# GpSimd's gate products: eight tensor_scalar instructions become two affine selections

## The chip, the cores and the metric

One NeuronCore of a Trainium2 chip runs the whole program. The metric is the device time of one execution in microseconds (us). The engines are TensorE (PE in the rows, PEld for its weight loads), VectorE (DVE), ScalarE (ACT), GpSimd (POOL) and SyncE (SP, which here only issues DMAs).

## The reference

`x` is `[8, 256, 256]` f32. The output is `x + attention(norm(x)) + experts(norm(x))`.

```python
# gated delta rule, 32 value heads, 16 key heads, chunks of 128 tokens; g is the log of the decay
g = -exp(A_log) * softplus(a + dt_bias)
def step(state, (q_t, k_t, v_t, g_t, b_t)):
    state = state * exp(g_t)
    delta = (v_t - state^T k_t) * b_t
    state = state + k_t delta^T
    return state, state^T q_t
y = rmsnorm(out * silu(z)) * norm_w @ w_out
# experts: 8 heads, the best 8 of 2048 experts for each token and head
z = silu((h . down_embed[indices]) * softmax(sc))
out = sum(z * up_embed[indices])
```

The kernel does not step through tokens: inside a chunk of 128 tokens it needs the matrix of decays `exp(g_{j+1} + ... + g_i)` for every pair of tokens. The exponent is made by one matrix product per four tasks: a constant triangle of ones (`C_GT`, row index greater than column index) times the matrix `gm[p, i] = g_p if p <= i else 0`. This `gm` is what the change is about.

## The kernel before

A first stage (up to about 284 us) normalises `x`, runs the dense part of the experts, finds the experts' indices and computes the gates `gates[:, 3, ...]`, which hold g for all tokens. Then come 64 passes. Pass `n` (with `f = n + 1`) does two things at once: the front half of the attention for group `f` (four head pairs' chunks, eight tasks `a`, each a 128x128 matrix), and the back half for group `n`, together with 16 expert slots of one tile of 128 tokens: a gather of 16 rows per token and the products with them.

Each engine has its own instruction list, in the order of the program text; they meet through semaphores. What matters here in one pass:

- GpSimd, `one_pass` of `block.gpsimd`: copies `cols2` (L964) and `xr` (L966), then, once TensorE has read the last `gm` (semaphore `diff_t`), `gate_sums(f + 1)` (L935 copies eight columns of g to `gn`; L939 makes the eight matrices of `gm`, a constant triangle `mask(C_LE)` times a column of `gn`). Then it waits for VectorE's third masked level (`e_v`, 3), copies the 16 indices (`picks`, L943) and `h2c` (L973), issues eight indirect DMAs (`gather(0)`, L952), scales the attention's output (`finish`, L928 and L931), waits for `mix_v`, issues the other eight gathers, computes `norm` (L980) and `MT` (L984, two instructions).
- VectorE, `one_pass` of `block.vector`: waits until all 16 rows have landed (`gathered`), runs 16 `expert_dot` (L1193: `rows` times `h2c`, summed; each is followed by a read of the accumulator), `zc` (L1299), the second half of the outputs (L1153, L1147), the masked level 0 (L1165 twice), part of the weighted sum of rows (L1204, L1207, L1210), three convolution taps (L1177), and the masked level 1 (L1165), whose first instruction raises `e_v` to 3.
- TensorE's `differences(g)` (L527) reads `gm` at the beginning of the next pass, after `gm_p` has reached its last value.

So `gm` is made one pass ahead, in a stretch in which VectorE is at the dot products.

Of the kernel before, what the change touches and what calls it, by code (L numbers as in the profile page):

```python
# [33 lines left out]
ALU = mybir.AluOpType  # L34
# [3 lines left out]
P = 128  # L38
# [6 lines left out]
TASKS = 8  # L45
# [13 lines left out]
C_ID, C_LE, C_GT, C_SU, C_EYE, C_MS = 0, 1, 2, 3, 4, 6  # L59
# [20 lines left out]
def program(nc, x, wkq, wvz, ckq, cvv, woh, wba, dtb, alog, nw, wup, bup, wdn, bdn, wq, keys, table, consts, out):  # L80
    ctx = ExitStack()
    with ctx:
        def sb(name, shape, dt=F32):
            return ctx.enter_context(nc.sbuf_tensor(name, shape, dt))

        def sem(name):
            return ctx.enter_context(nc.semaphore(name))
# [9 lines left out]
        h2_all = sb("h2_all", [P, TILES, P])  # L97
# [5 lines left out]
        def mask(c, n=1):  # L103
            m = cst[:, c * P:(c + 1) * P]
            return m if n == 1 else m.unsqueeze(1).broadcast_to([P, n, P])
# [29 lines left out]
        def diagonal(s):  # L135
# [7 lines left out]
                 "diff_t exp_done kk_t ss_t v_t e_t x_t xt_t proj_t y0_t s_t o0_t ks_t y1_t o1_t "  # L143
                 "yt_t out_t silu_s sq_s rv_s x_s xt_s tap_s z_s S_s qs_s sumsq_s yT_s "
                 "km_v kq_v ssk_v s_v at_v e_v conv_v ys0_v r1_v ys1_v xg_v acc_v rms_v elim_v dot_v "
                 "gn_p gm_p cols_p pick_p norm_p mt_p rms_p y_p zero_p scal_step silu_e sim_v mix_v "
                 "h2_s gate_v gate_s").split()
        sm = {n: sem(n) for n in names}
        nums = [s.num for s in sm.values()]
# [4 lines left out]
        class Step:  # L154
# [10 lines left out]
            def wait(self, n=None):  # L165
# [4 lines left out]
                   y1_t=1, o1_t=1, out_t=2, silu_e=1, exp_done=2, tap_s=8, x_s=4, xt_s=6, silu_s=4, sq_s=2, sumsq_s=8,  # L170
                   rv_s=8, S_s=1, qs_s=4, z_s=2, yT_s=2, dot_v=1, xg_v=4, e_v=6, conv_v=4, km_v=1, kq_v=1, ssk_v=2,
                   s_v=1, at_v=2, rms_v=1, mix_v=1, elim_v=1, ys0_v=2, ys1_v=2, r1_v=4, acc_v=2, cols_p=1, zero_p=1,
                   gn_p=1, gm_p=8, rms_p=1, y_p=8, pick_p=1, norm_p=1, mt_p=2, w_vz=32, xb_in=16, wo_in=16, w_kq=32,
                   blocks_out=32, blocks_in=16, inv_out=32, inv_in=64)
        place = {"u": 0}

        def at(name, n):

            return place["u"] * per[name] + n

        def last(name, n=None):

            return (place["u"] - 1) * per[name] + (per[name] if n is None else n)
# [55 lines left out]
        gn = sb("gn", [P, TASKS])  # L239
        gm = sb("gm", [P, TASKS, P])  # L240
# [51 lines left out]
        h2c = sb("h2c", [P, P])  # L292
# [5 lines left out]
        def task(b, c, r):  # L298
            return (2 * b + c) * R + r
# [104 lines left out]
        def _(pe):  # L404
# [99 lines left out]
            def one_pass(f, nx, back):  # L504
# [76 lines left out]

                if not back:
                    pe.wait_ge(loaded_kq, 32)
                    pe.wait_ge(sm["gm_p"], at("gm_p", 8))
                if place["u"] and front:
                    pe.wait_ge(sm["gm_p"], last("gm_p"))
                    pe.wait_ge(sm["z_s"], last("z_s", 1))
# [324 lines left out]
        def _(pool):  # L912
# [12 lines left out]
            def finish():  # L925

                pool.wait_ge(sm["rms_v"], at("rms_v", 1))
                pool.tensor_tensor(rms[:, :], rms[:, :], minus_half, ALU.pow).then_inc(sm["rms_p"], 1)  # L928
                pool.wait_ge(sm["rms_p"], at("rms_p", 1))
                for a in range(TASKS):  # L930
                    pool.tensor_scalar(xg[:, a, :], xg[:, a, :], rms[:, a:a + 1], None, ALU.mult).then_inc(sm["y_p"], 1)  # L931

            def gate_sums(f, calls=1):

                pool.tensor_copy(gn[:, :].rearrange("p (t r) -> p t r", t=4),  # L935
                                 gates[:, 3, bass.ds(4 * (f // HEADS), 4), bass.ds(R * (f % HEADS), R)]).then_inc(sm["gn_p"], 1)
                pool.wait_ge(sm["gn_p"], at("gn_p", calls))
                for a in range(TASKS):
                    pool.tensor_scalar(gm[:, a, :], mask(C_LE), gn[:, a:a + 1], None, ALU.mult).then_inc(sm["gm_p"], 1)  # L939

            def picks(f):

                pool.tensor_copy(pick[:, :], idx_all[:, bass.ds(f // 4, 1), bass.ds((f % 4) * 16, 16)].rearrange("p a c -> p (a c)"))\  # L943
                    .then_inc(sm["pick_p"], 1)

            def gather(k0):

                pool.wait_ge(sm["pick_p"], at("pick_p", 1))
                for k in range(k0, k0 + K // 2):
                    for s in range(2):  # L950
                        m = K * s + k
                        pool.indirect_dma_start(rows[:, m, :], None, table[:, :],  # L952
                                                bass.IndirectOffsetOnAxis(ap=pick[:, m:m + 1], axis=0)).then_inc(gathered, 16)

            def one_pass(f, nx, n):

                if f is None:
                    finish()
                    return
                hn, pn = f % HEADS, f // HEADS  # L960
                if place["u"]:
                    pool.wait_ge(sm["qs_s"], last("qs_s"))
                    pool.wait_ge(sm["inv_out"], last("inv_out"))
                pool.tensor_copy(cols2[nx][:, :, :].rearrange("p q (t r) -> p q t r", t=4),  # L964
                                 gates[:, 0:3, bass.ds(4 * pn, 4), bass.ds(R * hn, R)]).then_inc(sm["cols_p"], 1)
                pool.tensor_copy(xr[:, 0:BL * BL], cst[0:NB * TASKS, C_EYE * P:(C_EYE + 2) * P]).then_inc(sm["zero_p"], 1)  # L966
                pool.wait_ge(sm["diff_t"], at("diff_t", 2))
                if f + 1 < PASSES:
                    gate_sums(f + 1, 2 if n is None else 1)
                if n is not None:  # L970
                    pool.wait_ge(sm["e_v"], at("e_v", 3))
                picks(f)
                pool.tensor_copy(h2c[:, :], h2_all[:, bass.ds(f // 4, 1), :].rearrange("p a c -> p (a c)"))  # L973
                gather(0)
                if n is not None:
                    finish()
                    pool.wait_ge(sm["mix_v"], at("mix_v", 1))
                gather(K // 2)
                pool.wait_ge(sm["ssk_v"], at("ssk_v", 2))
                pool.tensor_tensor(norm2[nx][:, :], ss[:, :, :].rearrange("p w t -> p (w t)"), both, ALU.pow).then_inc(sm["norm_p"], 1)  # L980
                pool.wait_ge(sm["exp_done"], at("exp_done", 2))
                pool.wait_ge(sm["kq_v"], at("kq_v", 1))
                for g in range(2):
                    pool.tensor_tensor(MT2[nx][:, 4 * g:4 * g + 4, :].rearrange("p (t r) i -> p t r i", r=R),  # L984
                                       kq[:, 2 * g:2 * g + 2, :].unsqueeze(2).broadcast_to([P, 2, R, P]),
                                       DT[:, 4 * g:4 * g + 4, :].rearrange("p (t r) i -> p t r i", r=R), ALU.mult).then_inc(sm["mt_p"], 1)
# [23 lines left out]
        def _(dve):  # L1010
# [139 lines left out]
            def second_outputs(st, nx):  # L1150

                qs = QS[:, :, :].rearrange("p b d -> p (b d)")
                st.did(V.tensor_tensor(qs, ps[:, 4, :], qs, ALU.add))  # L1153
                st.wait()
                gated(1, qs, rq2[nx], z2[nx])

            def one_pass(nx, n, st, front=True):
# [5 lines left out]
                def level(lv, g):  # L1163
                    dve.wait_ge(sm["e_t"], at("e_t", 2 * lv + g + 1))
                    V.tensor_tensor(E[:, 4 * g:4 * g + 4, :], ps[:, g, :].rearrange("p (a i) -> p a i", a=4), mask(C_MS + lv, 4), ALU.mult)\  # L1165
                        .then_inc(sm["e_v"], 1)
# [25 lines left out]
                def expert_dot(k):  # L1192
                    st.did(V.tensor_tensor_reduce(out=rows[:, k, 0:P], in0=rows[:, k, 0:P], in1=h2c[:, :], scale=1.0, scalar=0.0,  # L1193
                                                  op0=ALU.mult, op1=ALU.add, accum_out=dot[:, k:k + 1]))
# [96 lines left out]
                if back:  # L1291
                    total = acc[:, bass.ds(n // 4, 1), :].rearrange("p a d -> p (a d)")
                    dve.wait_ge(gathered, 256 * n + 256)
                    for k in range(16):
                        expert_dot(k)

                    st.wait()
                    pr = prob_all[:, bass.ds(n // 4, 1), bass.ds((n % 4) * 16, 16)].rearrange("p a c -> p (a c)")
                    V.tensor_tensor(zc[:, 0, :], dot[:, :], pr, ALU.mult).then_inc(sm["dot_v"], 1)  # L1299
                    if place["u"]:  # L1300
                        dve.wait_ge(sm["o1_t"], last("o1_t"))
                        dve.wait_ge(sm["qs_s"], last("qs_s"))
                        dve.wait_ge(sm["z_s"], last("z_s"))
                        dve.wait_ge(sm["norm_p"], last("norm_p"))
                        dve.wait_ge(sm["mt_p"], last("mt_p"))
                    second_outputs(st, nx)
                    level(0, 0)
                    level(0, 1)
                    dve.wait_ge(sm["silu_e"], at("silu_e", 1))
                    expert_mix(0, 3)  # L1310
# [46 lines left out]
                if back:  # L1357
                    dve.wait_ge(sm["ks_t"], at("ks_t", 1))
                    for b in range(2):
                        for r in range(R):  # L1360
                            a = task(b, 1, r)
# [67 lines left out]
```

## Time and profile before

| | |
|---|---|
| median of 3 runs | 3440.19 us (3438.79 to 3451.68) |
| the profiled execution's own time | 3440.67 us |
| its span (first to last instruction) | 3438.8 us |
| busy: PE / PEld / DVE / ACT / POOL | 2992.4 / 2451.1 / 3012.3 / 1794.2 / 2306.0 us |
| POOL L939 `gm` | 512 instructions, 362.9 us |
| POOL L952 gathers | 1024 instructions, 1157.2 us |
| DVE L1193 dot products | 1024 instructions, 342.9 us |

The table gives busy time per engine and per group of instructions. Busy time says nothing of what a group delays: for that one needs the chain that ended last and, for one pass, the timelines of the two engines side by side.

### The profile page before, as it was taken

The page shows a single profiled execution, that of the slowest core. Times are in us where ns is not written, and L with a number is a line of the kernel's source. Part 1 is how long each engine was busy: PE and PEld are TensorE (multiplying, and loading weights), DVE is VectorE, ACT ScalarE, POOL GpSimd, SP SyncE. Part 2 cuts the span into 40 slices and gives each one's busy share as a digit, 9 for nine tenths or more (in the row PEclk, how much of TensorE's full clock was granted, in tenths as well). Part 3 has the DMA queues.
Part 4 walks back from the last instruction along what each step waited for, and adds up shares of the span by engine and source line. Part 5 has one row for each costly group of instructions (what it writes and reads, how often), then busy time and mean ns, then how long its engine had stood idle before and what let it go on. Part 6 is the DMA issues. An engine that isn't in the chain of part 4 may idle for free.

```text
span 3438.8 us, 56504 instructions
## 1 busy us (share of the span) xinstructions
PE 2992.4 (87%) x18444; PEld 2451.1 (71%) x18444; DVE 3012.3 (88%) x9101; ACT 1794.2 (52%) x4111; POOL 2306.0 (67%) x2650
## 2 busy tenths in 40 slices
PE   7844999989998989899989988898989899998997
PEld 4422777778776777677767777777777777777776
DVE  5996999989998999899989898998899898989996
ACT  3322555555554555455545555555555555555553
POOL 0005777777767776777778777877777667877764
PEclk9976999999999999999999999999999999999999
DMA  1003545544555545454545554544555454544553
GB/s 60 1 1 104 137 132 141 135 131 132 137 139 135 131 133 139 130 133 133 141 126 138 134 138 124 149 127 134 138 138 137 125 139 132 146 129 135 144 132 89
DMA packets 541827, 427.98 MB, mean 124 GB/s; under 512 B 247008, under 2 KB 450784, under 8 KB 541536
## 3 DMA queue, kind: packets, MB, share of 16 engines
q1 hardware_dynamic: 476000, 222.98, 24.0%
q0 software_dynamic: 65536, 201.39, 22.0%
q8 instruction: 149, 2.44, 0.3%
q14 instruction: 142, 1.16, 0.1%
HBM read 345.61 MB, written 45.09 MB: 114 GB/s over the span
## 4 chain that ended last, share of the span: by engine, by line
DVE 36%; POOL 35%; PE 14%; issue 9%; DMA 5%; ACT 1%; SPq 0%; DVEq 0%; POOLq 0%; ACTq 0%
POOL rows L952 22%; DVE rows L1193 9%; POOL xg L931 9%; DVE qkv L1177 6%; DVE mix L1210 4%; POOL rms L928 3%; DVE E L1165 3%; DMA rows<-table,pick 3%; PE ps L579 3%; PE ps L500 3%; PE ps L517 2%; PE ps L665 1%; DVE topi L1024 1%; DVE xg L1147 1%; PE ps L521 1%
## 5 line engine op out<-in xcount | busy, mean ns | idle before, releaser
L952 POOL DMA_INDIRECT rows<-table,pick x1024 | 1157.2, 1130 | 326.3 <-issue 326.3
L551 PE MATMUL ps<-X,AT 128*128 128x128 f32 x3072 | 417.7, 294 | 119.2 <-DMA XT<-whole 119.2
L551 PEld LDWEIGHTS ps<-X,AT 128*128 128x128 f32 x3072 | 392.9, 207 | 169.8 <-DMA XT<-whole 167.3
L806 ACT ACTIVATE qkv<-qkv 128x512 f32<-128x512 f32 x256 | 161.5, 631 | 518.6 <-DVE qkv L1177 518.6
L571 PE MATMUL ps<-XT,E 128*128 128x128 f32 x3072 | 400.6, 277 | 0.0
L801 ACT ACTIVATE raw<-ps 128x512 f32<-128x512 f32 x256 | 152.8, 597 | 433.2 <-PE ps L517 433.2
L1210 DVE SCALAR_TENSOR_TENSOR mix<-rows,zc,mix 128x256 f32<-128x256 f32 x896 | 375.1, 476 | 0.0
L571 PEld LDWEIGHTS ps<-XT,E 128*128 128x128 f32 x3072 | 368.9, 192 | 0.0
L939 POOL TENSOR_SCALAR gm<-cst,gn 128x128 f32<-128x128 f32 x512 | 362.9, 723 | 6.7
L1193 DVE CUSTOM_DVE_ANT_0 rows<-rows,h2c 128x128 f32<-128x128 f32 x1024 | 342.9, 399 | 9.2 <-SPq L328 4.7
L931 POOL TENSOR_SCALAR xg<-xg,rms 128x128 f32<-128x128 f32 x520 | 324.9, 637 | 7.0
L564 PEld LDWEIGHTS ps<-E,XT 128*128 128x128 f32 x2048 | 257.7, 193 | 98.1 <-DVE E L1165 56.5
L1177 DVE SCALAR_TENSOR_TENSOR qkv<-raw,cwv,qkv 128x510 f32<-128x510 f32 (+2 forms) x384 | 307.7, 802 | 6.8
L1177 DVE SCALAR_TENSOR_TENSOR qkv<-raw,cwkq,qkv 128x510 f32<-128x510 f32 (+2 forms) x384 | 285.7, 744 | 21.4 <-ACT qkv L802 12.1
L564 PE MATMUL ps<-E,XT 128*128 128x128 f32 x2048 | 274.1, 277 | 26.4 <-DVE E L1165 26.4
L943 POOL COPY pick<-idx_all 128x16 uint32<-128x16 uint32 x64 | 12.6, 196 | 421.9 <-DVE E L1165 421.9
L816 ACT ACTIVATE XT<-ps 128x512 f32<-128x512 f32 x384 | 228.0, 594 | 94.3 <-PE ps L571 86.4
L517 PE MATMUL ps<-xnT,Wkq 128*128 128x512 f32 x512 | 273.6, 661 | 0.0
L1165 DVE TENSOR_TENSOR E<-ps,cst 128x512 f32<-128x512 f32 x384 | 253.2, 682 | 14.6 <-PE ps L551 9.1
L517 PE MATMUL ps<-xnT,Wvz 128*128 128x512 f32 x512 | 254.2, 622 | 0.0
L500 PE MATMUL ps<-wo,yT 128*128 128x256 f32 x1040 | 247.6, 382 | 0.0
L521 PE MATMUL ps<-Wvz,xb 128*128 128x256 f32 x1024 | 243.1, 381 | 0.0
(167 smaller groups left out, 6333.4 us busy)
## 6 DMA issues: line engine op xcount, KB each, us to landing
Wvz<-wvz SPq DMA_DIRECT2D x64, 512.0 KB, 3.3
xb<-xnT SPq DMA_DIRECT2D x64, 512.0 KB, 4.4
whole<-AT SPq DMA_DIRECT2D x128, 256.0 KB, 3.6
X<-whole SPq DMA_DIRECT2D x128, 256.0 KB, 3.9
XT<-whole SPq DMA_DIRECT2D x128, 256.0 KB, 4.4
wo<-woh SPq DMA_DIRECT2D x65, 256.0 KB, 4.4
Wkq<-wkq SPq DMA_DIRECT2D x64, 256.0 KB, 2.5
rows<-table,pick POOLq DMA_INDIRECT x1024
```

What stands on the lines that cost most here:

```text
L500: done = mm(ps[:, 2 + g, c * D:(c + 1) * D], yT[:, task(g, c, r), :], wo[:, r, :], start=r == 0, stop=r == R - 1)
L517: done = mm(ps[:, bank, :], w[:, k, :], xnT[:, k, bass.ds(pn * N, N)], start=k == 0, stop=k == KD - 1)
L551: done = mm(ps[:, g, (a % 4) * P:(a % 4 + 1) * P], AT_b[:, a, :], src[:, a, :], start=True, stop=True)
L564: done = mm(ps[:, 2 + g, (a % 4) * P:(a % 4 + 1) * P], src[:, a, :], E[:, a, :], start=True, stop=True)
L571: done = mm(ps[:, 4 + g, (a % 4) * P:(a % 4 + 1) * P], E[:, a, :], src[:, a, :], start=True, stop=True)
L931: pool.tensor_scalar(xg[:, a, :], xg[:, a, :], rms[:, a:a + 1], None, ALU.mult).then_inc(sm["y_p"], 1)
L939: pool.tensor_scalar(gm[:, a, :], mask(C_LE), gn[:, a:a + 1], None, ALU.mult).then_inc(sm["gm_p"], 1)
L952: pool.indirect_dma_start(rows[:, m, :], None, table[:, :], bass.IndirectOffsetOnAxis(ap=pick[:, m:m + 1], axis=0)).then_inc(gathered, 16)
L1165: V.tensor_tensor(E[:, 4 * g:4 * g + 4, :], ps[:, g, :].rearrange("p (a i) -> p a i", a=4), mask(C_MS + lv, 4), ALU.mult)\
L1177: ins = V.scalar_tensor_tensor(out=o, in0=i, scalar=w, in1=o, op0=ALU.mult, op1=ALU.add)
L1193: st.did(V.tensor_tensor_reduce(out=rows[:, k, 0:P], in0=rows[:, k, 0:P], in1=h2c[:, :], scale=1.0, scalar=0.0, op0=ALU.mult, op1=ALU.add, ...
L1210: sums[s] = st.did(V.scalar_tensor_tensor(out=mix[:, s, :], in0=rows[:, m, P:ROW], scalar=zc[:, 1, m:m + 1], in1=mix[:, s, :], op0=ALU.mul ...
```

## The change

`gate_sums` fills the same `gm` with two instructions in place of eight. Each takes four columns of `gn`, broadcasts every one over 128 columns (a stride of zero), and keeps the element where `column - partition >= 0`, else writes 0. The constant triangle is no longer read. The semaphore `gm_p` rises by 2 in a pass in place of 8. A register for the fill value is set once ahead of the passes. GpSimd's copy to `h2c` now raises a semaphore `h2c_p`, and VectorE waits for its value of the pass before, ahead of the dot products.

```diff
@@ block.gpsimd
+            zero = pool.to_reg(0.0)
             def gate_sums(f, calls=1):
                 pool.tensor_copy(gn[:, :].rearrange("p (t r) -> p t r", t=4),
                                  gates[:, 3, bass.ds(4 * (f // HEADS), 4), bass.ds(R * (f % HEADS), R)]).then_inc(sm["gn_p"], 1)
                 pool.wait_ge(sm["gn_p"], at("gn_p", calls))
-                for a in range(TASKS):
-                    pool.tensor_scalar(gm[:, a, :], mask(C_LE), gn[:, a:a + 1], None, ALU.mult).then_inc(sm["gm_p"], 1)
+                for g in range(2):
+                    pool.affine_select(gm[:, 4 * g:4 * g + 4, :], gn[:, 4 * g:4 * g + 4].unsqueeze(2).broadcast_to([P, 4, P]),
+                                       [[0, 4], [1, P]], ALU.is_ge, zero, base=0, channel_multiplier=-1).then_inc(sm["gm_p"], 1)
@@ one_pass
-                pool.tensor_copy(h2c[:, :], h2_all[:, bass.ds(f // 4, 1), :].rearrange("p a c -> p (a c)"))
+                pool.tensor_copy(h2c[:, :], h2_all[:, bass.ds(f // 4, 1), :].rearrange("p a c -> p (a c)")).then_inc(sm["h2c_p"], 1)
@@ block.tensor, one_pass
-                    pe.wait_ge(sm["gm_p"], at("gm_p", 8))
+                    pe.wait_ge(sm["gm_p"], at("gm_p", 2))
@@ block.vector, one_pass
                     dve.wait_ge(gathered, 256 * n + 256)
+                    if place["u"]:
+                        dve.wait_ge(sm["h2c_p"], last("h2c_p"))
                     for k in range(16):
                         expert_dot(k)
```

## Rows read from the trace of the kernel before

**Rows 1.** The page: span, busy time of each engine, shares of the chain.

```profile
span 3438.8 us, 56504 instructions
...
DVE 36%; POOL 35%; PE 14%; issue 9%; DMA 5%; ACT 1%; SPq 0%; DVEq 0%; POOLq 0%; ACTq 0%
```

**Rows 2.** GpSimd's waits: waiter <- releaser: us in total, times, longest.

```profile
POOL pick L943 <- DVE E L1165: 421.9, 63, 13.2
```

**Rows 3.** The chain in 2025 to 2045 us: start, us, what.

```profile
2025.08 4.12 DMA rows<-table,pick
...
2034.84 0.06 DVE zc L1299
...
2034.95 0.05 DVEq L1305
...
2043.23 0.61 DVE E L1165
```

**Rows 4.** GpSimd's timeline of the same pass: start, us, instruction, idle before.

```profile
2028.15 2.48 POOL L984 TENSOR_TENSOR MT<-kq,DT 128x512 f32<-128x512 f32 x2
2030.59 0.19 POOL L964 COPY cols<-gates 128x24 f32<-128x24 f32 x1
2030.74 0.39 POOL L966 COPY xr<-cst 64x256 f32<-64x256 f32 x1
...
2031.43 5.74 POOL L939 TENSOR_SCALAR gm<-cst,gn 128x128 f32<-128x128 f32 x8
2043.90 0.20 POOL L943 COPY pick<-idx_all 128x16 uint32<-128x16 uint32 x1 [6.73 <-DVE E L1165]
```

**Rows 5.** VectorE's timeline of the same pass.

```profile
2027.81 1.28 DVE L1142 TENSOR_TENSOR acc<-acc,ps 128x512 f32<-128x512 f32 x2
2029.22 2.06 DVE L1193 CUSTOM_DVE_ANT_0 rows<-rows,h2c 128x128 f32<-128x128 f32 x1
...
2031.63 0.28 DVE L1193 CUSTOM_DVE_ANT_0 rows<-rows,h2c 128x128 f32<-128x128 f32 x1
...
2031.85 0.36 DVE L1193 CUSTOM_DVE_ANT_0 rows<-rows,h2c 128x128 f32<-128x128 f32 x1
...
2034.01 0.36 DVE L1193 CUSTOM_DVE_ANT_0 rows<-rows,h2c 128x128 f32<-128x128 f32 x1
```

**Rows 6.** GpSimd's groups by shape: busy us, mean ns.

```profile
L939 POOL TENSOR_SCALAR gm<-cst,gn 128x128 f32<-128x128 f32 x512 | 362.9, 723 | 6.7
L984 POOL TENSOR_TENSOR MT<-kq,DT 128x512 f32<-128x512 f32 x128 | 159.2, 1260 | 0.0
L966 POOL COPY xr<-cst 64x256 f32<-64x256 f32 x64 | 24.8, 387 | 0.0
L973 POOL COPY h2c<-h_all 128x128 f32<-128x128 f32 x64 | 18.8, 293 | 0.0
```

**Rows 7.** VectorE's groups by shape.

```profile
L1142 DVE TENSOR_TENSOR acc<-acc,ps 128x512 f32<-128x512 f32 x130 | 83.1, 679 | 12.3 <-PE ps L500 12.3
L1147 DVE SCALAR_TENSOR_TENSOR xg<-QS,norm,z 128x256 f32<-128x256 f32 x130 | 65.0, 539 | 2.3
L1147 DVE SCALAR_TENSOR_TENSOR xg<-ps,norm,z 128x256 f32<-128x256 f32 x128 | 56.0, 479 | 197.5 <-PE ps L579 197.5
L1153 DVE TENSOR_TENSOR QS<-ps,QS 128x512 f32<-128x512 f32 x65 | 45.0, 692 | 2.4 <-issue 0.4
```

**Rows 8.** L939: duration ns min/median/max, first and last start.

```profile
L939 POOL TENSOR_SCALAR gm<-cst,gn x512: 595/738/1131, 284.4 to 3296.0; 128x128 f32<-128x128 f32 x171
```

**Rows 9.** GpSimd's timeline of a longer pass, and VectorE's first dot product there.

```profile
2088.15 5.45 POOL L939 TENSOR_SCALAR gm<-cst,gn 128x128 f32<-128x128 f32 x8
2099.16 0.20 POOL L943 COPY pick<-idx_all 128x16 uint32<-128x16 uint32 x1 [5.57 <-DVE E L1165]
...
2086.44 0.28 DVE L1193 CUSTOM_DVE_ANT_0 rows<-rows,h2c 128x128 f32<-128x128 f32 x1
```

**Rows 10.** The chain in 280 to 336 us, ahead of the passes.

```profile
284.44 4.67 POOL gm L939 x8
```

More of the change, by code:

```diff
@@ L145, in program @@
                  "km_v kq_v ssk_v s_v at_v e_v conv_v ys0_v r1_v ys1_v xg_v acc_v rms_v elim_v dot_v "
-                 "gn_p gm_p cols_p pick_p norm_p mt_p rms_p y_p zero_p scal_step silu_e sim_v mix_v "
+                 "h2c_p gn_p gm_p cols_p pick_p norm_p mt_p rms_p y_p zero_p scal_step silu_e sim_v mix_v "
                  "h2_s gate_v gate_s").split()
@@ L172, in program @@
                    s_v=1, at_v=2, rms_v=1, mix_v=1, elim_v=1, ys0_v=2, ys1_v=2, r1_v=4, acc_v=2, cols_p=1, zero_p=1,
-                   gn_p=1, gm_p=8, rms_p=1, y_p=8, pick_p=1, norm_p=1, mt_p=2, w_vz=32, xb_in=16, wo_in=16, w_kq=32,
+                   h2c_p=1, gn_p=1, gm_p=2, rms_p=1, y_p=8, pick_p=1, norm_p=1, mt_p=2, w_vz=32, xb_in=16, wo_in=16, w_kq=32,
                    blocks_out=32, blocks_in=16, inv_out=32, inv_in=64)
```

## The prediction

> **What bounds the kernel now.** I read the page first for the span and the shares of the chain, then GpSimd's waits, then the chain of one pass in the middle, and at last the timelines of GpSimd and VectorE over that pass, side by side. The chain belongs to two engines in turn, VectorE with 36% and GpSimd with 35% [rows 1]. The waits show how they take turns: 63 times, once a pass, GpSimd stands still for 421.9 us in all until VectorE's masked level is written, and only then copies the indices [rows 2]. In the pass read here the gather's data lands at 2029.20 [rows 3], VectorE's first dot product starts at 2029.22 [rows 5], VectorE works without a real gap to the end of the masked level at about 2043.85 [rows 3], and GpSimd's index copy starts at 2043.90 [rows 4]. From there GpSimd carries the chain again (gathers, output scaling, gathers). So a pass is a loop of a VectorE stretch and a GpSimd stretch.
>
> The eight gate products lie in neither. They run on GpSimd from 2031.43 to 2037.17, while VectorE has the turn, and behind them GpSimd is idle for 6.73 us [rows 4]. Their own 362.9 us [rows 6] are therefore not on the path. What they can change is how fast VectorE gets through its stretch, and that is the whole question here.
>
> **What GpSimd does to VectorE in that stretch.** The first dot product took 2.06 us where its neighbours take 0.28 [rows 5]. It ended at 2031.28, so it really ran from 2031.00. From 2029.22 to 2031.00 it was held, while GpSimd was in its two MT instructions (to 2030.63), the copy of cols and the copy of xr (to 2031.13) [rows 4]. Two things follow. A GpSimd instruction that reads this memory holds a VectorE instruction with two such inputs (rows and h2c). And it isn't let in between GpSimd instructions that follow each other closely: the two copies have one input each, and still kept it out 0.37 us after MT's end. Instructions of VectorE that take one input from PSUM don't suffer: the two additions to acc, from 2027.81, lay largely beside MT and took 1.28 us together [rows 5], no more than their group's mean of 679 ns each, and QS<-ps,QS, of the same shape, has 692 though it lies beside the gate products [rows 7].
>
> The gate products hold VectorE only a little: in this pass four of the dot products took 0.36 in place of 0.28, one for each gate product that ran beside them (at 2031.85, 2032.57, 2033.29 and 2034.01; the first and the last stand in [rows 5]). One gate product takes 595 ns at least [rows 8], but costs VectorE only 0.08; most of it is spent on something else than reading 128 elements.
>
> The Trainium skill has a rule for this, on the page "SBUF — State Buffer", section "SBUF: two separate sides": GpSimd and VectorE lock a shared pair of ports, one excludes the other for the whole instruction, and a VectorE instruction with two SBUF inputs is one that needs it. The MT rows agree (held 1.78 us); the gate products' rows don't agree as to the whole instruction (0.08 of 0.6 us). By the rule to the letter, eight products held it for their whole length and two selections would hold it for less, which speaks for the change; by the rows it speaks against.
>
> **The change part by part.**
>
> 1. Taken out: what the eight products cost VectorE in its stretch. Four dot products by 0.08 is 0.32. The two xg instructions have a mean of 539 ns with QS as source, and 479 with PSUM as source in another place of the pass [rows 7]: 2 x 0.06 = 0.12. Together 0.45 us a pass. There are 512/8 = 64 sets of products, two of them ahead of the first pass (the first at 284.4), so 62 passes gain: 62 x 0.45 = 28 us.
>
> 2. Put in: what two selections of 512 elements cost VectorE. The trace has no affine selection on any engine, so I bound it. They begin where the products began, 2031.43, and there are 12 or 13 dot products left (zc follows them at 2034.84 [rows 3]), each with two inputs, so everything that the pair holds hits VectorE. Length from below: a copy on GpSimd takes 293 ns for 128 elements and 387 for 256, so 0.73 ns an element and 0.2 us fixed [rows 6]; at 512 it would be 0.57 us, 1.15 for the pair. From above: MT, also 512 elements written but with two inputs, takes 1.26 [rows 6], or 2.5 for the pair; per element (1.26 - 0.2)/512 = 2.07 ns. The selection reads one input as the copy does, but has to form an index and compare for each element. I take the middle of the two rates, 1.4 ns: 0.2 + 0.72 = 0.91 us, 1.83 for the pair. As with MT, cols and xr I take it that VectorE isn't let in between the two; the dot product that is already running at the start gives back about 0.2. So VectorE is held for 1.65 us a pass (with the copy's rate 0.95, with MT's 2.3).
>
> The Trainium skill prices such a loop: "GPSIMD Engine Reference", section "Performance pitfalls for Q7 kernels", gives 2.03 cycles an element for compare and select, not unrolled, at the 1.2 GHz of its "Specifications". As an estimate from that page this is 0.87 us for 512 elements, 1.07 with the fixed 0.2, and the sum below would come to about 3530 us. No row here shows it.
>
> 3. Net: 1.65 - 0.45 = +1.20 us in a pass. All of it lands on the path, since VectorE's stretch has no gap to take it up and GpSimd's index copy waits for its end: 62 x 1.20 = +74 us. In the few longer passes, as the one at 2086, the products begin 1.71 us after the first dot product [rows 9]; eight or nine dot products are still to come, so it holds there too.
>
> 4. GpSimd ends gate_sums earlier, by 5.74 - 1.83 = 3.9 us. Nothing waits for that: its idle time before the index copy grows from 6.7 to about 11.8 us (6.7 + 3.9 + 1.2). TensorE reads gm only in the next pass.
>
> 5. Ahead of the first pass the eight products are on the chain once, with 4.67 us [rows 10]. The pair needs 1.83: -2.8 us. The second set there has its length hidden by the front half of the first pass.
>
> 6. The wait for h2c_p asks for a copy of the pass before, long done. It stands behind the wait for the gather, ahead of the first dot product. Another step of VectorE's queue on the chain costs 0.05 us [rows 3]; in the usual pass the first dot product is held by MT until 2031.00 anyway, which hides it. Without that cover it would be 63 x 0.05 = 3 us; I put in 0. Setting the register for zero once: 0. TensorE's wait for 2 in place of 8 asks for the same moment.
>
> Sum, against the profiled execution's own time: 3440.67 + 74 - 2.8 = 3512 us. The median of the runs shown, 3440.19, is 0.5 below it, so this is also the forecast for the median. With the copy's rate: 0.95 - 0.45 = 0.50, x 62 = 31, less 3.5: 3468. With MT's: 1.85 x 62 = 115, less 2.2: 3553.
>
> **The rivals.**
>
> A. The selection holds VectorE only for a read at the rate seen with the products, 0.08 us for each 128 elements, and lets it in between. Then 8 x 0.08 = 0.64 against 0.45: +0.19 x 62 = +12, less 2.8, or 3450 us. For it: the products are of that kind, 0.6 us long and holding for a seventh of that. Against it: MT and both copies were not.
>
> B. The selection doesn't hold VectorE at all, or no longer than the products did for the whole set, because it makes most of its values itself and its input is only four numbers a partition. VectorE gets back the 0.45 us: -28 - 3 = 3410 us, faster. It decides wherever the pair holds VectorE for less than 0.45 us. For it: the input has a stride of zero. Against it: the copy of xr, a plain one-input instruction, held it nearly to its end.
>
> C. The selection is a slow loop, slower than MT. If it takes what four products take without contention, 4 x 0.595 = 2.4 us [rows 8], and holds the port for it, VectorE loses 4.5 us a pass: 4.05 x 62 = +251, or about 3690 us. For it: tensor_scalar with a column as its scalar takes 595 ns for 128 elements, far above a copy's 293, so GpSimd's loops differ much. Against it: much of that seems to be fixed cost. GpSimd's own slack decides only beyond 5.74 + 6.73 = 12.5 us for the pair [rows 4], which I leave out.
>
> D. That the products are gone from GpSimd and the time falls because GpSimd is 35% of the chain: excluded, since the idle time behind them is there in the usual pass and in the longer one (6.73 and 5.57 us) [rows 4, 9].
>
> **How the numbers follow.** Within 0.5% (17 us) counts as no change here, about what a measurement of this kernel can tell. The forecast (pair held for between 0.95 and 2.3 us) has a chance of 0.60, with a range of its own of 3465 to 3555; A 0.15; B 0.13; C with all between MT's rate and it 0.12. Faster: B, 0.13. Same: A without its slower end, 0.14. Slower: 0.60 + 0.12 and A's rest, 0.73. The range leaves out B (0.13) and the upper part of C (0.07), and reaches from 3438 to 3620 us. The predicted time is that of the forecast, 3512.
>
> **What would show it.** In the profile after: a selection's mean between 0.57 and 1.26 us; GpSimd's wait for VectorE's masked level up from 421.9 to about 740 us (63 waits, about 5 us each more); in a usual pass one or two dot products besides the first that last 0.8 to 2 us, and the other dot products all at 0.28; xg<-QS at about 480 ns; the stretch from the first dot product to the index copy longer by 1.2 us, and the stretch from there to the next gather's landing unchanged. The forecast is wrong if no dot product besides the first is over 0.4 us (then B or A), if the held dot products add up to more than 2.5 us a pass (C), or if VectorE's stretch grows and the span doesn't, which would mean that the loop isn't closed as I read it.

## The result, and the profile after

The changed kernel takes 3471.17 us (median of 5 runs, 3469.07 to 3483.47), the kernel before 3442.12 in the same comparison. The ratio is 1.0088, with a 95% interval of 1.0064 to 1.0112: slower by 29 us, where the forecast was slower by 71. The sign and the place are as predicted, the size isn't.

The page of the changed kernel: span, busy time of each engine.

```profile
span 3473.8 us, 56184 instructions
PE 3002.3 (86%) x18444; PEld 2449.5 (71%) x18444; DVE 3041.1 (88%) x9101; ACT 1796.4 (52%) x4111; POOL 2022.8 (58%) x2266
```

GpSimd got 283 us less to do (2306.0 before) and the kernel got slower. Its waits show where the 283 us went:

```profile
POOL pick L946 <- DVE E L1168: 721.2, 63, 12.4
```

It was 421.9 [rows 2], so GpSimd waits 299 us more. The next two fences are the timelines of GpSimd and of VectorE in one usual pass; they answer to [rows 4] and [rows 5].

```profile
2051.75 2.49 POOL L987 TENSOR_TENSOR MT<-kq,DT 128x512 f32<-128x512 f32 x2
2054.19 0.19 POOL L967 COPY cols<-gates 128x24 f32<-128x24 f32 x1
2054.34 0.39 POOL L969 COPY xr<-cst 64x256 f32<-64x256 f32 x1
2054.68 0.24 POOL L937 COPY gn<-gates 128x8 f32<-128x8 f32 x1
2055.00 1.27 POOL L941 TENSOR_SCALAR_AFFINE_SELECT gm<-gn 128x512 f32<-128x512 f32 x2
2067.94 0.20 POOL L946 COPY pick<-idx_all 128x16 uint32<-128x16 uint32 x1 [11.67 <-DVE E L1168]
```

```profile
2052.74 2.15 DVE L1196 CUSTOM_DVE_ANT_0 rows<-rows,h2c 128x128 f32<-128x128 f32 x1
2054.81 0.28 DVE L1196 CUSTOM_DVE_ANT_0 rows<-rows,h2c 128x128 f32<-128x128 f32 x1
2055.02 0.76 DVE L1196 CUSTOM_DVE_ANT_0 rows<-rows,h2c 128x128 f32<-128x128 f32 x1
2055.71 0.70 DVE L1196 CUSTOM_DVE_ANT_0 rows<-rows,h2c 128x128 f32<-128x128 f32 x1
2056.35 0.28 DVE L1196 CUSTOM_DVE_ANT_0 rows<-rows,h2c 128x128 f32<-128x128 f32 x1
```

The pair lasts 1.27 us, and beside it stand exactly two long dot products, 0.76 and 0.70 in place of 0.28: 0.48 + 0.42 = 0.90 us held. All later ones take 0.28. The first of the two ends at 2055.78, while GpSimd's pair is still running, so VectorE does get in between the two selections; the second ends 0.14 us behind the pair. GpSimd then idles for 11.67 us. In the groups by shape, the xg instructions with QS as source took 539 ns before [rows 7] and take 484 now, nearly the 479 of those with PSUM as source; QS<-ps,QS, which has one input from PSUM, took 692 ns and takes 691:

```profile
L1150 DVE SCALAR_TENSOR_TENSOR xg<-QS,norm,z 128x256 f32<-128x256 f32 x130 | 57.6, 484 | 2.3
L1156 DVE TENSOR_TENSOR QS<-ps,QS 128x512 f32<-128x512 f32 x65 | 44.9, 691 | 2.8 <-issue 0.8
```

To follow this through all passes I cut each of the 62 passes that make a gm at two moments that can be read in any timeline: the end of the first dot product, and the start of GpSimd's index copy. Between them lies VectorE's stretch, from there to the next pass's first dot product lies GpSimd's.

| | VectorE's stretch, median | sum over 62 | GpSimd's stretch, median | sum over 62 |
|---|---|---|---|---|
| before | 12.62 us | 785.1 | 34.94 us | 2219.7 |
| changed | 13.06 us | 811.5 | 34.97 us | 2221.4 |

VectorE's stretches account for 26.4 us and GpSimd's for 1.7. The profiled execution is 35 us longer than the one before; most of the rest, 8 us, lies ahead of the first pass, where TensorE's granted clock had a mean of 0.86 in the first 100 us against 1.00 in the execution before. In another profile of the changed kernel (below) that clock is 1.00 and the first dot product ends 9.6 us earlier. Over all thirteen profiles of this document the first dot product ends at 331 to 335 us where that clock is 1.00, at 339 to 342 where it is 0.93, and at 342 and 343 where it is 0.86, whatever the kernel. So these 8 us belong to the execution and not to the change.

### The profile page after: what moved, and what is told of

Read it like the earlier page. It is cut to its first block, busy times and chain, and to the rows that moved or that the text cites. A ratio compares the mean times of both kernels' runs of the same rounds, so it can differ in the third digit from the quotient of the medians.

```text
span 3473.8 us, 56184 instructions
## 1 busy us (share of the span) xinstructions
PE 3002.3 (86%) x18444; PEld 2449.5 (71%) x18444; DVE 3041.1 (88%) x9101; ACT 1796.4 (52%) x4111; POOL 2022.8 (58%) x2266
## 3 DMA queue, kind: packets, MB, share of 16 engines
q14 instruction: 140, 1.15, 0.1%
## 4 chain that ended last, share of the span: by engine, by line
DVE 37%; POOL 36%; PE 12%; issue 10%; DMA 5%; ACT 0%; DVEq 0%; SPq 0%; POOLq 0%; ACTq 0%
POOL rows L955 23%; DVE rows L1196 10%; POOL xg L931 9%; DVE qkv L1180 6%; DVE mix L1213 4%; DMA rows<-table,pick 4%; DVE E L1168 3%; POOL rms L928 3%; PE ps L500 2%; PE ps L579 2%; PE ps L517 2%; DVE topi L1027 1%; DVE QS L1156 1%; DVE xg L1150 1%; PE ps L665 1%
## 5 line engine op out<-in xcount | busy, mean ns | idle before, releaser
L946 POOL COPY pick<-idx_all 128x16 uint32<-128x16 uint32 x64 | 12.7, 198 | 721.2 <-DVE E L1168 721.2
L1196 DVE CUSTOM_DVE_ANT_0 rows<-rows,h2c 128x128 f32<-128x128 f32 x1024 | 373.9, 429 | 11.6 <-SPq L328 5.6
L517 PE MATMUL ps<-xnT,Wkq 128*128 128x512 f32 x512 | 265.6, 644 | 0.0
L1150 DVE SCALAR_TENSOR_TENSOR xg<-ps,norm,z 128x256 f32<-128x256 f32 x128 | 56.0, 479 | 204.8 <-PE ps L579 204.8
```

Of the source, the lines that this page charges most:

```text
L517: done = mm(ps[:, bank, :], w[:, k, :], xnT[:, k, bass.ds(pn * N, N)], start=k == 0, stop=k == KD - 1)
```

## Experiments

Theory P is the prediction's, with its size put right by the profile: two selections hold VectorE's two-input instructions for 0.45 us each, where the products cost 0.45 us for the whole set. Rival W: the cost is the new semaphore and wait. Rival L: GpSimd's instruction list falls differently, and more passes are long ones. In every seventh or so of the passes GpSimd stands still for 4 to 6 us ahead of one of its indirect DMAs, for no reason that the profile shows (longest 6.1 us). In the pass of [rows 9], which follows such a stop, VectorE reaches its first dot product at 2086.44, when MT and the two copies have been over since 2082.68. I count a pass as long where the first dot product isn't held, that is, takes under 0.4 us: 8 of 62 before, 11 in the changed kernel.

Beside the first eight experiments the kernel before takes about 3500 us, beside the last three 3447. The number of the chip doesn't tell the two groups apart: it is 3 for four of the eight (the wait alone, one column, late selections, late products) and for the last three, and 9 for the other four. The cause of the difference is open. In the slower group all kernels have a GpSimd stretch of 35.6 to 35.8 us, 0.7 more than above, and 21 to 28 long passes. VectorE's median stretch is the same in both groups where the two can be compared (12.62 for the kernel before and for the wait alone), which makes it the better measure; its sum over the 62 passes stands beside it, since a median hides a minority of longer passes. "Held" is what the 15 later dot products of a pass take above 0.28 us, median over the passes.

| | ratio to before (95%) | VectorE's stretch, median | sum over 62 | held |
|---|---|---|---|---|
| before (again) | 0.9989 (0.9974 to 1.0003) | 12.62 | 784.7 | 0.34 |
| changed (again) | 1.0076 (1.0058 to 1.0093) | 13.07 | 810.9 | 0.90 |
| wait alone | 1.0012 (0.9988 to 1.0035) | 12.62 | 782.2 | 0.34 |
| selections of one column | 0.9952 (0.9929 to 0.9975) | 12.19 | 766.1 | 0.04 |
| eight selections of 128 | 1.0082 (1.0052 to 1.0112) | 12.86 | 798.2 | 0.70 |
| one selection of 1024 | 1.0100 (1.0070 to 1.0131) | 13.09 | 815.2 | 0.93 |
| three selections of 512 | 1.0227 (1.0195 to 1.0259) | 13.49 | 845.1 | 1.33 |
| products late | 0.9958 (0.9934 to 0.9983) | 12.38 | 770.6 | 0.01 |
| selections late | 0.9917 (0.9886 to 0.9949) | 12.22 | 762.1 | 0.05 |
| selections late, again | 0.9949 (0.9926 to 0.9973) | 12.21 | 759.8 | 0.00 |
| selections and copies late | 0.9906 (0.9891 to 0.9922) | 12.22 | 778.2 | 0.00 |

**The wait alone.** The kernel before with the semaphore only.

```diff
-                pool.tensor_copy(h2c[:, :], ...)
+                pool.tensor_copy(h2c[:, :], ...).then_inc(sm["h2c_p"], 1)
                     dve.wait_ge(gathered, 256 * n + 256)
+                    if place["u"]:
+                        dve.wait_ge(sm["h2c_p"], last("h2c_p"))
```

> The kernel before with nothing of the change but its semaphore: GpSimd's copy to h2c raises h2c_p, VectorE waits for it ahead of the dot products. Theory P (the two selections hold VectorE's dot products for about 0.45 us each, 0.90 a pass, where the eight products and their effect on xg cost 0.45 a pass): the wait is hidden, 3442 us, ratio to before 0.999 to 1.001, spans and dot products as before (four of 0.36 us a pass). Rival W (the new wait and semaphore are the cost): about 3470 us, ratio 1.008. Rival L (the list of GpSimd's instructions falls differently, so that more passes are long ones, 11 against 8): 3442, since its list is as before.

Measured 1.0012, an interval across 1, and VectorE's stretch is 12.62 us as before. W falls.

**Selections of one column.** Every instruction and semaphore of the change, nearly nothing to read.

```diff
+                w = P if n is None else 1
                 for g in range(2):
-                    pool.affine_select(gm[:, 4 * g:4 * g + 4, :], gn[:, 4 * g:4 * g + 4].unsqueeze(2).broadcast_to([P, 4, P]),
-                                       [[0, 4], [1, P]], ...)
+                    pool.affine_select(gm[:, 4 * g:4 * g + 4, 0:w], gn[:, 4 * g:4 * g + 4].unsqueeze(2).broadcast_to([P, 4, w]),
+                                       [[0, 4], [1, w]], ...)
```

> The changed kernel, but inside the passes each of the two selections fills one column of each of its four matrices in place of 128; the rest of gm is left as it was (this leaves out the fill of the later passes, so the decays are wrong). All instructions and semaphores stay. Theory P: nothing holds the dot products any more, they all take 0.28 us but the first of a pass, VectorE's stretch is 0.90 us shorter than in the changed kernel and 0.45 shorter than before: 3442 - 28 - 3 = 3411 us, ratio 0.991. W and L: as the changed kernel, about 3470, ratio 1.008.

VectorE's stretch is 12.19 us, 0.43 below before and 0.87 below the changed kernel: this is the stretch with nearly nothing beside it (held 0.04), and it gives both terms of the sum. The products cost 12.62 - 12.19 = 0.43 us a pass, the two selections 13.06 - 12.19 = 0.87. The time fell by less than the 27 us that this is worth (62 x 0.43): the ratio is 0.9952, and 0.991 lies outside its interval. In its profile VectorE's stretches add up to 766 us, 16 below the 782 of the wait alone, since 12 of its 62 passes have one of 12.5 us or more (up to 14.5); GpSimd's add up to 2297 us against 2277, with 26 long passes against 23. So a part of the gain was given back on both sides; why stays open.

**Eight selections of 128, and one of 1024.** The same elements in other pieces; the same instruction, once with `for a in range(TASKS)` over `gm[:, a, :]`, once over all of `gm`.

```diff
-                for g in range(2):
-                    pool.affine_select(gm[:, 4 * g:4 * g + 4, :], gn[:, 4 * g:4 * g + 4].unsqueeze(2).broadcast_to([P, 4, P]), [[0, 4], [1, P]], ...)
+                for a in range(TASKS):
+                    pool.affine_select(gm[:, a, :], gn[:, a:a + 1].broadcast_to([P, P]), [[1, P]], ...)
```

> The changed kernel with eight selections of 128 columns in place of two of 512: the same elements, the same input. Theory P1 (what holds VectorE is the time that a selection reads, at one element a cycle or about 0.83 ns, 0.43 us for 512): each lasts about 0.3 us and holds by up to 0.11; together 0.6 to 0.9 us a pass, VectorE's stretch 12.8 to 13.1 us, ratio 1.005 to 1.009. Rival P2 (a selection holds nearly from its start to its end, fixed part included, 0.2 of 0.64 us more each): 8 x 0.3 = up to 2 us a pass, stretch 14 us, ratio above 1.02.

> The changed kernel with one selection of 1024 columns. Theory P1: 1.07 us long (0.2 + 1024 x 0.83 ns), one dot product held by 0.85 to 0.90 us, no other; stretch 13.0 to 13.1 us as with two, ratio 1.007 to 1.009. If reading ahead into a queue frees VectorE before the selection ends, the hold is well under 0.85 us and the ratio under 1.005.

The selections' own lines (duration ns min/median/max), first of the changed kernel, then with 128 and with 1024 columns:

```profile
L941 POOL TENSOR_SCALAR_AFFINE_SELECT gm<-gn x128: 636/641/682, 292.7 to 3327.6; 128x512 f32<-128x512 f32 x128
```

```profile
L941 POOL TENSOR_SCALAR_AFFINE_SELECT gm<-gn x512: 287/337/520, 290.1 to 3389.5; 128x128 f32<-128x128 f32 x171
```

```profile
L940 POOL TENSOR_SCALAR_AFFINE_SELECT gm<-gn x64: 1091/1091/1097, 290.2 to 3413.6; 128x1024 f32<-128x1024 f32 x64
```

From 512 to 1024 elements a selection grows by 0.45 us, 0.88 ns an element; about 0.19 us are fixed. VectorE beside the one of 1024, and then beside the eight of 128:

```profile
2090.61 1.21 DVE L1195 CUSTOM_DVE_ANT_0 rows<-rows,h2c 128x128 f32<-128x128 f32 x1
2091.76 0.28 DVE L1195 CUSTOM_DVE_ANT_0 rows<-rows,h2c 128x128 f32<-128x128 f32 x1
```

```profile
2090.29 0.41 DVE L1196 CUSTOM_DVE_ANT_0 rows<-rows,h2c 128x128 f32<-128x128 f32 x1
...
2090.93 0.36 DVE L1196 CUSTOM_DVE_ANT_0 rows<-rows,h2c 128x128 f32<-128x128 f32 x1
```

One dot product held by 0.93, or eight of them by 0.08 (the first by 0.13). Theory P1 had expected 0.85 to 0.90 for the one, and up to 0.11 each for the eight; both stretches lie in their ranges, and the stretch of 14 us of P2 falls. The ratio of the 1024, 1.0100, is just above its range. For the eight the ratio of 1.0082 is higher than the stretch of 12.86 is worth: (12.86 - 12.62) x 62 is 15 us, or 0.4%.

Which part of a selection holds isn't settled by this. P1 says its reading part, about 0.9 us per 1024 elements: that is 0.93 of 1.09 us for the one, and 0.11 where 0.08 of 0.29 was measured for each of the eight. But a hold up to the selection's end, with one dot product let in between two selections, fits as well or better. The selection of 1024 runs from 2090.59 to 2091.68 and the held dot product ends 0.14 us later, and so it is beside the selections of 512 and of 128: the median over their held dot products is 0.14 us each time. Free dot products follow each other every 0.21 us (2054.81, 2055.02 above). If each selection costs its own length less one such step, that gives 1.09 - 0.21 = 0.88, 0.64 - 0.21 = 0.43 and 0.29 - 0.21 = 0.08 us, where 0.93, 0.45 and 0.08 were measured. P2 had left out the dot product let in. No run separates the two accounts, and both give nearly the same price.

This shows also that a product isn't cheaper to VectorE than a selection of the same size: one of 128 elements holds by 0.08 [rows 5], as a selection of 128 does. Of a product, though, most lets VectorE through: beside each of the first four products in the pass of [rows 4], 0.72 to 0.88 us long, there are three or four dot products, and only one of them is held. What differed between eight products and eight selections is how they lay. The products were spread over 5.7 us, from 2031.43 to 2037.17, and the last ones fell beside these VectorE instructions of before, of which QS and E have an input from PSUM; the eight selections lie in 2.35 us, all beside dot products.

```profile
2035.05 0.69 DVE L1153 TENSOR_TENSOR QS<-ps,QS 128x512 f32<-128x512 f32 x1
2035.77 1.01 DVE L1147 SCALAR_TENSOR_TENSOR xg<-QS,norm,z 128x256 f32<-128x256 f32 x2
2036.70 1.27 DVE L1165 TENSOR_TENSOR E<-ps,cst 128x512 f32<-128x512 f32 x2
```

**Three selections of 512.** A third one into a buffer that nobody reads.

```diff
+                if n is not None:
+                    if place["u"]:
+                        pool.wait_ge(sm["ex_p"], last("ex_p"))
+                    pool.affine_select(gx[:, :, :], gn[:, 0:4].unsqueeze(2).broadcast_to([P, 4, P]),
+                                       [[0, 4], [1, P]], ...).then_inc(sm["ex_p"], 1)
```

> The changed kernel with a third selection of 512 columns behind the two in every pass, into a buffer that nobody reads. GpSimd has over 11 us of idle time for it. Theory P, with what the first runs showed (a selection of 512 columns lasts 0.64 to 0.66 us and holds one dot product by 0.45): three held dot products a pass in place of two, VectorE's stretch from the end of the first dot product to GpSimd's index copy 13.51 us in place of 13.06, the whole 28 us above the changed kernel, ratio to before about 1.017. If the cost is no matter of the selections (W, L): ratio 1.008 and a stretch of 13.06.

```profile
2120.64 0.76 DVE L1202 CUSTOM_DVE_ANT_0 rows<-rows,h2c 128x128 f32<-128x128 f32 x1
2121.33 0.70 DVE L1202 CUSTOM_DVE_ANT_0 rows<-rows,h2c 128x128 f32<-128x128 f32 x1
2121.96 0.70 DVE L1202 CUSTOM_DVE_ANT_0 rows<-rows,h2c 128x128 f32<-128x128 f32 x1
```

Three held dot products, and a stretch of 13.49 us where 13.51 was expected. The ratio, 1.0227, is above the 1.017 expected, outside its interval. Its profile has 28 long passes against 22 in the second one of the late selections (below), taken on the same chip, and its GpSimd stretches add up to 2303 us against 2281. In this group of runs a longer VectorE stretch costs somewhat more than its own length; the cause is open.

**Late.** GpSimd has over 11 us of slack behind the selections, so they may be moved to where VectorE has an input from PSUM. One wait does that, for the selections and, in a kernel of its own, for the eight products of before:

```diff
                 pool.wait_ge(sm["gn_p"], at("gn_p", calls))
+                if n is not None:
+                    pool.wait_ge(sm["xg_v"], at("xg_v", 2))
```

> The changed kernel, with one more wait on GpSimd: the two selections of a pass (not the copy of gn ahead of them) wait until VectorE has written both of its second outputs xg (xg_v, 2), so that they lie beside the two masked levels E<-ps, which take one input from PSUM and last 1.2 us together. Theory P: dot products at 0.28, xg at 0.48, the levels unaffected, the first mix instruction held by 0.1 to 0.2 us: 3442 - 28 - 3 + 9 = 3420 us, ratio 0.991 to 0.995, faster than both. W and L: about 3470. If GpSimd holds every VectorE instruction and not only those with two inputs in SBUF: 3470 too, with E<-ps at 0.9 to 1.1 us.

GpSimd and VectorE with the late selections:

```profile
2069.40 1.23 POOL L943 TENSOR_SCALAR_AFFINE_SELECT gm<-gn 128x512 f32<-128x512 f32 x2 [5.14 <-DVE xg L1152]
2076.43 0.20 POOL L948 COPY pick<-idx_all 128x16 uint32<-128x16 uint32 x1 [5.80 <-DVE E L1170]
```

```profile
2068.38 0.88 DVE L1152 SCALAR_TENSOR_TENSOR xg<-QS,norm,z 128x256 f32<-128x256 f32 x2
2069.18 1.28 DVE L1170 TENSOR_TENSOR E<-ps,cst 128x512 f32<-128x512 f32 x2
2070.37 0.53 DVE L1209 SCALAR_TENSOR_TENSOR mix<-rows,zc,acc 128x256 f32<-128x256 f32 x1
```

The same two selections, the same wait for h2c, and the cost is gone: the two E take 1.28 us as in the changed kernel, where nothing lay beside them, and only the end of the second selection holds a mix, 0.53 against 0.47. Stretch 12.22, ratio 0.9917. W can't give that, and L says nothing of a shorter VectorE stretch (the long passes are 22, about as many as the 23 of the wait alone). A hold of every VectorE instruction is excluded too.

> The two selections made to wait for VectorE's second outputs, once more, to see if it beats both kernels again: stretch 12.22 us against 12.62 before and 13.06 changed, 62 x 0.40 = 25 us and 3 us ahead of the passes: ratio to before 0.992, with 0.988 to 0.996 allowed for runs in which more passes are long ones.

Again faster: 0.9949, stretch 12.21.

> The kernel before, with the same wait ahead of its eight products. They last 4.8 to 5.7 us and so cannot hide beside the two levels of 1.2 us. Theory P: the dot products are free (0.32 us gained), xg too (0.12), but about six products run beside mix and the convolution taps and cost 0.08 to 0.1 us each: 3435 to 3445 us, ratio 0.998 to 1.001. If products cost VectorE nothing beside those instructions: 3414. The late gm itself has no price: GpSimd has 6.7 us of idle time there and uses about 5.5 of it.

```profile
L941 POOL TENSOR_SCALAR gm<-cst,gn x512: 592/800/1154, 284.0 to 3349.6; 128x128 f32<-128x128 f32 x171
```

The dot products are free (held 0.01), the stretch is 12.38: the products still cost 12.38 - 12.19 = 0.19 us beside mix and the taps, less than expected (six products at 0.08 to 0.1, about 0.5). The mix group's mean went from 476 to 507 ns, but the three taps beside them took 0.77, 0.75 and 0.75 us, two of them as undisturbed. The ratio is 0.9958 where 0.998 to 1.001 was expected; 62 x 0.24 = 15 us, or 0.4%, is what the stretch is worth. GpSimd pays instead: its median product went from 738 ns [rows 8] to 800.

**Selections and copies late.** The first dot product of a usual pass is held by MT, cols and xr. The two copies can wait as well.

```diff
+                if n is not None:
+                    pool.wait_ge(sm["dot_v"], at("dot_v", 1))
                 pool.tensor_copy(cols2[nx][:, :, :] ...
```

> The late selections, and the copies of cols and xr wait too, until VectorE's dot products are done (dot_v), so that they lie beside QS<-ps,QS, which has an input from PSUM. Theory P: the first dot product of a usual pass is let in at the end of MT, not 0.37 us behind it, so the stretch from GpSimd's index copy to the end of the first dot product is 0.3 to 0.4 us shorter in the passes where MT holds it (40 of 62 or so), the stretch behind it stays 12.22: 15 us below the late selections, ratio to before 0.988 to 0.991. Rival: the copies are not what keeps the dot product out, it needs 0.37 us to start behind MT: ratio 0.992 to 0.995 as with the late selections alone.

```profile
2019.71 2.49 POOL L991 TENSOR_TENSOR MT<-kq,DT 128x512 f32<-128x512 f32 x2
2025.91 0.20 POOL L971 COPY cols<-gates 128x24 f32<-128x24 f32 x1 [3.72 <-DVE zc L1308]
2026.06 0.39 POOL L973 COPY xr<-cst 64x256 f32<-64x256 f32 x1
2027.53 1.23 POOL L943 TENSOR_SCALAR_AFFINE_SELECT gm<-gn 128x512 f32<-128x512 f32 x2 [0.94 <-DVE xg L1154]
```

```profile
2020.79 1.56 DVE L1200 CUSTOM_DVE_ANT_0 rows<-rows,h2c 128x128 f32<-128x128 f32 x1 [0.16 <-DMA rows<-table,pick]
```

MT ends at 2022.20, the dot product at 2022.35; before it ended 0.65 us behind MT. GpSimd's stretch has a median of 34.52 us against 34.94 in the kernel before in the same group of runs, and its sum is 2194 us against 2218. The ratio is 0.9906, 3418.38 us against 3447.32: faster than both kernels, and inside the range expected.

The number came out, but not all of its working. VectorE's median stretch is 12.22, yet the sum is 778.2 us, only 6.5 below the 784.7 of before, where 62 x 0.40 = 25 were expected: 28 of the 62 passes have a stretch of 12.5 us or more, up to 15.6. In these passes VectorE has to wait: ahead of the taps for ScalarE's qkv (21.0 us in 23 waits, where the first profile of the kernel before has 12.1 in three, 11.5 of it in one), and ahead of E for TensorE (15.1 us against 9.1). Whether the late copies or the shorter pass brings these waits on is open. The late selections alone were not run in this group, so what the copies add to them in time isn't measured.

**Both kernels again, side by side.**

> The kernel before, run under a name of its own, for a profile on the chip of this call: the other runs were made on chips on which it takes about 3500 us in place of 3442. Theory P: VectorE's stretch is 12.62 us as in its first profile, since port holds don't depend on the chip; GpSimd's stretch is about 35.6 to 35.7 us in place of 34.9, as in all kernels profiled there, and more of the passes are long ones. Ratio 1.000. If rival L were right, the number of long passes would be 8 here and 11 or more in the changed kernel on the same chip.

> The changed kernel on the same chip as the others of this call. Theory P: stretch of VectorE 13.06 us, ratio to before 1.006 to 1.010; the number of long passes within 3 of that of the kernel before. L: several long passes more than before, and a VectorE stretch that accounts for less than half of the difference.

The kernel before takes 3442 us here, as in the first comparison, and its GpSimd stretch is 34.94 and not the 35.6 expected. VectorE's stretches are 12.62 and 13.07, their sums 784.7 and 810.9: 26.2 us. The long passes are 8 and 10, GpSimd's stretches add up to 2218 and 2228 us. So L isn't nothing: two or three passes more are long, and GpSimd's stretches are 1.7 us longer in the first pair of profiles and 10 in this one. But VectorE's stretch carries most of the difference in both pairs.

## Why the prediction was right and wrong

**What bounds the kernel, and where the change acts: right.** Chain of two stretches, the gate products in neither, GpSimd's slack not worth anything, all of the cost as holds of VectorE's dot products. GpSimd's wait was forecast to grow to about 740 us, it grew to 721.2 (see steps 4 to 6 for how much that says).

**Step 1, what the products cost (0.45 us a pass): right.** 0.43 by the one-column kernel, and both of its parts: the dot products were held 0.34 in all, and xg<-QS lost 55 ns each.

**Step 2, what the selections cost (1.65 us a pass): wrong, it is 0.87.** Two choices failed, both in the same direction. I took the length from the middle of two rates, 0.91 us; it is 0.64, close to the copy's rate (0.57 at 512 elements) and far from MT's. And I took it that VectorE is shut out between the two selections, as it was between MT, cols and xr. It wasn't: it finished one dot product there, worth 0.21 us. The length of the pair, 1.83 forecast and 1.27 measured, makes 0.56 of the missing 0.78 us, the dot product let in 0.21.

The selection has one input in SBUF as the copy has, and what it does with it (index, compare) cost little time per element: 0.88 ns, where the copy's rows give 0.73 and MT's 2.07. The bound from the copy, worked out in the prediction as 0.95 us a pass and 3468 us, was 3 us from the median of 3471. That close it came by luck, since its pair was too short (1.15 us) and its hold without a dot product let in too long. The nearest row was the one with the same number of inputs, and I weighed it equally with one that reads twice as much.

Measured, a selection takes 0.88 ns an element, which at 1.2 GHz is 1.06 cycles. The Trainium skill, "GPSIMD Engine Reference", section "Performance pitfalls for Q7 kernels", states 2.03 cycles for compare and select and 1.03 if unrolled by two; the trace agrees with the second figure, and the 3530 us estimated from the first was too high. The rule of the Trainium skill on "SBUF — State Buffer", section "SBUF: two separate sides", that the pair of ports is locked for the whole instruction, agrees with this case in which VectorE instructions are held (two inputs in SBUF, not those with one from PSUM). It doesn't agree for the products (0.08 us of a row of 0.6 or more). For the selections the held dot product does end 0.14 us behind the selection, but one dot product gets in between each two, so the rows don't decide.

**Step 3, that all of it lands on the path: right.** 62 x 0.44 = 27 us by the stretches' medians, against 62 x 1.20 = 74. These 47 us are more than the whole error of the time (3512 against 3471, 41 us).

**Steps 4 to 6: right, in part by construction.** The idle time is 11.67 us (11.8 forecast). This says little for step 2: a longer pair would end GpSimd's work later and VectorE's stretch by as much, so its length cancels. GpSimd ended 4.5 us earlier and not 3.9, VectorE's stretch grew by 0.44 and not 1.2; the two errors cancel nearly, and so they do in the 740. The wait costs nothing (the wait alone, 1.0012). Ahead of the first pass the pair lasts about 1.25 us in place of 4.67; that gain of some 3 us can't be seen in the profiles, since that stage varies by 8 us from one to the next.

**Rivals.** A (0.08 per 128 elements, VectorE let in between) said 3450 us; the rate of its hold was right, the 0.64 us that it gives is what eight pieces cost (0.67), and two long ones cost 0.2 more. It was nearer to the measured time (21 us off) than the forecast was (41). B and C didn't occur.

**The range** of 3438 to 3620 us held the time, but it was so wide that it left out little, not even an unchanged kernel. The forecast's own, 3465 to 3555, held it near its lower end, at the copy's bound. The rise was forecast as 71 us and measured as 29, and step 2 is the reason.

## What to carry to other kernels

Work that an engine does in its slack isn't free if it holds up instructions of the engine that has the turn, and making it shorter can make the kernel slower: what counts is what it is beside. Look for the instructions of the critical engine that aren't held (here those with an input from PSUM), and hang the other engine's work on the semaphore that starts them; here that one wait turned a loss of 0.8% into a gain of 0.5 to 0.8%. Check the sums over all passes too, and not one pass or a median alone: with the copies late as well, VectorE began to wait for other engines in 28 of 62 passes. Where an operation isn't in the trace, take its price from the row with the same operands, not from the mean of unlike ones.

## What the runs showed that I had not expected

- GpSimd's hold of VectorE's dot products went with the elements that the instruction beside them makes, 0.6 to 0.9 ns each, for products and selections alike: 0.08 us for 128 (product or selection), 0.45 for 512, 0.93 for 1024. In a product the other part, some 0.5 us, lets VectorE through; for a selection's 0.2 us that isn't shown.
- A product of 128 elements with a column as its scalar (592 ns at least) takes twice as long as a selection of 128 (287).
- Two small copies behind MT (cols and xr) kept the first dot product out: it ended 0.64 us behind MT, and 0.15 when they were moved beside QS, which still takes 0.69 us. GpSimd's stretch fell by 0.42 us. They may have a price elsewhere, since VectorE's stretches add up to 778 us and not to 62 x 12.22 = 758.
- The same kernel took 3442 us in some runs and 3500 in others, the longer time with GpSimd's stretch 0.7 us longer and 20 or so long passes in place of 8, on chips of the same number. VectorE waited 9.1 us for TensorE ahead of E in the profile of before, and 85.6 in that of the wait alone. The holds are the same in both.
